# Two PSUM copies per pass of an expert loop go from ScalarE to VectorE (one Trainium2 core)

## What is computed

```python
S, R, M, K = (8, 16, 64, 4)          # 8 groups, rank 16, 64 experts per group, 4 chosen
z = jnp.einsum('nd,sdr->nsr', xf, P)
scores = jnp.einsum('nsr,smr->nsm', z, C)      # 8 x 64 = 512 scores per row
topv, topi = jax.lax.top_k(scores, K)
w = jax.nn.softmax(topv, axis=-1)
h = jax.nn.gelu(jnp.einsum('nsr,nskrh->nskh', z, W1g) + b1g)
yl = jnp.einsum('nskh,nskhr->nskr', h, W2g) + b2g
comb = jnp.einsum('nskr,nsk->nsr', yl, w)
out = jax.nn.gelu(comb @ G1 + g1b) @ G2 + g2b
```

## Time and profile before

| what | value |
|---|---|
| median of 3 runs | 939.27 us (939.06 to 944.86) |
| the profiled execution, its own time | 939.98 us |
| its span (first to last instruction) | 938.2 us, so 1.8 us lie around it |
| granted TensorE clock, mean | 0.981 of full speed |
| PE busy | 881.2 us, 94% |
| DVE busy | 670.1 us, 71% |
| ACT busy | 592.1 us, 63% |
| POOL busy | 478.7 us, 51% |

### The profile page before, as it was taken

How to read it: one execution, slowest core, us unless ns; L and a number is a source line. 1 busy time by engine, 2 the same in 40 slices (tenths; PEclk the granted TensorE clock), 3 DMA queues, 4 the chain that set the end, 5 groups by cost and what they waited for, 6 DMA issues and landing times.

```text
span 938.2 us, 16131 instructions
## 1 busy us (share of the span) xinstructions
PE 881.2 (94%) x5408; PEld 397.9 (42%) x5408; DVE 670.1 (71%) x1678; ACT 592.1 (63%) x871; POOL 478.7 (51%) x448
## 2 busy tenths in 40 slices
PE   8799999999999968899989998999999999999997
PEld 3477777777777756122222222222222222222222
DVE  5566666665675866777787878787878887877774
ACT  1121211223333245788898999899989998988784
POOL 0335353334243517477766666666656665665453
PEclk9999999999999988699999999999999999999999
DMA  9500000000000166966878798878788987899772
GB/s 250 219 1 1 1 37 36 1 1 1 1 1 21 39 112 107 257 227 212 237 243 241 233 253 252 250 243 252 229 266 227 264 236 239 245 259 288 234 254 101
DMA packets 89804, 154.14 MB, mean 164 GB/s; under 512 B 30211, under 2 KB 56068, under 8 KB 89329
## 3 DMA queue, kind: packets, MB, share of 16 engines
q1 hardware_dynamic: 88750, 149.86, 53.1%
q10 hardware_dynamic: 972, 3.24, 2.7%
HBM read 138.81 MB, written 15.83 MB: 165 GB/s over the span
## 4 chain that ended last, share of the span: by engine, by line
PE 71%; DVE 11%; ACT 11%; issue 4%; DMA 1%; POOL 1%; SPq 0%; ACTq 0%; DVEq 0%; POOLq 0%
PE ps L797 15%; PE ps L734 14%; PE ps L450 8%; PE ps L458 5%; PE ps L523 4%; PE ps L773 4%; PE ps L515 3%; DVE ring L1557 3%; PE ps L532 3%; DVE ring L1560 3%; PE ps L574 2%; PE ps L493 2%; PE ps L545 2%; ACT ring L1105 2%; ACT ring L1112 2%
## 5 line engine op out<-in xcount | busy, mean ns | idle before, releaser
L1761 POOL TENSOR_TENSOR ring<-ring,wbc 128x512 f32<-128x512 f32 x192 | 244.9, 1281 | 155.4 <-ACT ring L1112 137.9
L1557 DVE TENSOR_TENSOR ring<-ps,ring 128x1024 f32<-128x1024 f32 x192 | 234.6, 1222 | 92.5 <-ACT ring L1105 50.8
L734 PE MATMUL ps<-zst,w1st 99*128 99x512 bf16 x768 | 218.7, 389 | 23.0 <-ACT ring L1105 15.0
L797 PE MATMUL ps<-ring,w2cur 128*32 128x512 f32 x1536 | 204.8, 606 | 0.0
L1105 ACT ACTIVATE ring<-ps 128x1024 f32<-128x1024 f32 x192 | 197.3, 1027 | 6.4 <-PE ps L734 6.2
L1616 POOL TENSOR_TENSOR t<-t 128x768 f32<-128x768 f32 x48 | 87.4, 1833 | 187.7 <-DVE t L1243 187.7
L1114 ACT ACTIVATE ps<-ps 128x512 f32<-128x512 f32 x192 | 114.1, 594 | 45.1 <-PE ps L734 44.8
L1560 DVE TENSOR_TENSOR ring<-ps,wbc 128x512 f32<-128x512 f32 x192 | 130.9, 682 | 2.2 <-DMA wbc<-w_rows 2.2
L734 PEld LDWEIGHTS ps<-zst,w1st 99*128 99x128 bf16 x768 | 60.2, 98 | 162.4 <-issue 36.8
L1241 DVE TENSOR_TENSOR t<-ps,rope 128x768 f32<-128x768 f32 x48 | 45.7, 952 | 104.7 <-PE ps L458 68.5
L1112 ACT ACTIVATE ring<-ps 128x512 f32<-128x512 f32 x192 | 115.6, 602 | 0.3 <-PE ps L734 0.3
(11 more groups left out here) (169 smaller groups left out, 1153.6 us busy)
## 6 DMA issues: line engine op xcount, KB each, us to landing
wbc<-w_rows SPq DMA_DIRECT2D x192, 512.0 KB, 5.2
w2cur<-in_w SPq DMA_DIRECT2D x48, 256.0 KB, 5.0
w_parts<-wp SPq DMA_DIRECT2D x72, 64.0 KB, 3.3
zst<-z_parts SPq DMA_DIRECT2D x72, 64.0 KB, 5.3
w1st<-w_parts ACTq DMA_DIRECT2D x12, 256.0 KB
wst<-w_parts SPq DMA_DIRECT2D x24, 128.0 KB, 4.5
z_parts<-zp SPq DMA_DIRECT2D x6, 384.0 KB, 5.0
wst<-w_parts SPq DMA_DIRECT2D x24, 96.0 KB, 4.7
```

The source lines that it names most:

```text
L734: return pe.matmul(bank(to), w1st[0:99, 4 * a + j, col:col + P], zst[0:99, (i // 2) % 2, j, :], start=True, stop=True)
L797: mm = pe.matmul(bank(YBANK, 0, 512, 32 * j, 32 * j + 32), w2cur[:, n, j, :], ring[:, (4 * g + j) % RING, :], start=False, stop=(n == 7 an ...
L1557: dve.tensor_tensor(v, ps[:, WBANK * 512:WBANK * 512 + 1024], v, ALU.mult).then_inc(s["duo_done"], 1)
L1761: pool.tensor_tensor(ring[:, slot, :], ring[:, slot, :], wbc[:, g % 4, 1, :], ALU.mult).then_inc(s["tri_done"], 1)
```

## The change

Both copies are removed from ScalarE's loop. In VectorE's loop the scores of the next tile are copied at n = 4 and the transposed weights at n = 6, each behind the two products of the group, and the weights' copy ahead of `largest`. The waits of the copies go with them. What runs before the loop (tiles 0 to 5) keeps its copies on ScalarE.

```diff
@@ ScalarE's loop @@
                                ACT.Gelu_apprx_tanh).then_inc(s["duo_gelu"], 1)
-                if n == 6 and tile < TILES:
-                    keep_gates(tile, PBANK)
                 if g >= 18 and g % 16 == 2:
...
                     ln_root(5, 12, 24)
-                if n == 4 and tile + 1 < TILES:
-                    copy_scores(tile + 1, PBANK)
@@ VectorE @@
+            def copy_scores(tile, at):
+
+                dve.wait_ge(s["s_full"], tile + 1)
+                dve.wait_ge(s["t_mr"], LENT + tile)
+                dve.wait_ge(s["p_dist"], LENT + tile)
+                dve.tensor_copy(sc[:, :, 0:M], bank(at).rearrange("p (s m) -> p s m", m=M)).then_inc(s["s_copied"], 1)
+
+            def keep_gates(tile, at):
+
+                dve.wait_ge(s["t_full"], tile + 1)
+                if tile >= 8:
+                    dve.wait_ge(s["r_stored"], 32 * (tile - 7))
+                    dve.wait_ge(s["lo_done"], LENT + tile - 7)
+                dve.tensor_copy(gates_of(tile), bank(at).rearrange("p (g n) -> p g n", g=4)).then_inc(s["wT_done"], 1)
@@ VectorE's loop @@
                     normaliser(tile)
+                if n == 4 and tile + 1 < TILES:
+                    copy_scores(tile + 1, PBANK)
+                if n == 6 and tile < TILES:
+                    keep_gates(tile, PBANK)
                 if n in (5, 6) and tile + 1 < TILES:
                     largest(tile + 1, 4 * (n - 5), 4 * (n - 4))
```

## The result

| | before | changed |
|---|---|---|
| median | 942.07 us (939.06 to 945.04, 4 runs) | 958.42 us (956.64 to 959.94, 4 runs) |
| profiled execution, span | 939.98 us, 938.2 us | 958.0 us, 956.2 us |
| DVE / ACT busy | 670.1 / 592.1 us | 696.8 / 574.9 us |

The ratio is 1.0174, 95% interval [1.0134, 1.0214]: slower by 16.3 us, where +0.7% was forecast. The direction was right, the size was not, and the range (up to 951.5) was missed.

What follows compares the result with a forecast made beforehand. TensorE was taken as the bound, with VectorE setting the pace from group 7 to 1. Costs by pass, 4.1 + 1.4 + 0.2 + 0.8 - 0.25 = 6.2 us, gave a median of 945.5 us (+0.7%), range 938.5 to 951.5.

Steps and rivals of the forecast that it cites:

- The bounds: TensorE bounds except at three waits; from group 7 to 1 VectorE works back to back and sets the pace.
- Part 1, what ScalarE gives: Without ScalarE's copies, TensorE's matmuls lose waits of 0.12 us at group 4 and 0.27 at group 6 per plain pass.
- The copy's duration and pitch: A moved 128x512 copy on VectorE: 0.68 us long, 0.60 from start to start, bounds 0.33 and 0.74.
- The group 4 copy: Score copy behind line 1560 of group 4, hidden in 0.59 us of VectorE idle time: cost 0.
- The signs by busy time: Signs of a right forecast: ScalarE's busy time down by 21.9 us, VectorE's up by about 37 x 0.68 = 25.
- The sum by kinds of pass: Costs added over the loop's plain, pre-`first_final`, early and last passes: 6.2 us in all.
- the passes up to a `first_final`: Passes 4, 8, 12 and 16, where VectorE catches up behind the first wait: 0.35 us each, 1.4 in all.
- pass 0's 0.8: Pass 0, group 4: two small additional VectorE operations leave too little idle time; estimated at twice a plain pass, 0.8 us.
- Pass 18: VectorE idles 1.05 us at group 6 and takes the copy free; TensorE keeps its gain: -0.25 us.
- the group 6 item of part 2: Gate copy ahead of the maxima on VectorE adds 0.60 us, so line 1557 of group 7 starts 0.41 late.
- The GpSimd item: `high_part` starts at the copy's end, 572.9, and group 7's product is 0.36 us late, needed over 3 us later: cost 0.
- Clearly slower: Rival: relief doesn't reach VectorE at group 6 and the group 4 copy shows, or all copies are bare: 950.7 to 961.5, chance 0.09.

Runs made afterwards that it cites:

- e1_again: Second run of the changed kernel with VectorE's small top4 copy written as a tensor_reduce over an axis of one element: 951.13 us, ratio 1.0099.
- e3: The changed kernel with the group 6 gate copy back on ScalarE, so only the group 4 score copy is on VectorE: ratio 0.9987.
- before_again: The kernel before, unchanged, run once more for a second profile: ratio 1.0028 to the kernel before.
- e8: e1_again's kernel with TensorE's idle gap ahead of group 4 of passes 3, 7, 11 and 15 filled by repeated score matmuls: 949.03 us, ratio 1.0072.
- after_again: The changed kernel, unchanged, run a second time beside e1_again: 956.10 us, ratio 1.0159.
- e7: e3's kernel with ScalarE's group 6 gate copy moved behind the tri gelu: 955.39 us, ratio 1.0133.
- e5: The changed kernel with GpSimd's high_part moved from group 6 to group 7, ahead of low_parts: ratio 1.0189.
- e12: e7's kernel with the small copy as a tensor_reduce and the idle gap of passes 3, 7, 11 and 15 filled: 936.56 us, ratio 0.9934.

## Why the prediction was wrong

By its own steps:

- **The bounds: right.** VectorE sets the pace from group 7 to group 1. With the reduce (e1_again) TensorE gives the relief back ahead of `duo_gates` of group 0, 0.50 us, and 0.2 us behind it; the forecast had `two_first` of groups 0 and 2.
- **Part 1, what ScalarE gives: right.** 0.12 us per plain pass at group 4 (e3: 22.20 - 22.09 = 0.11), 0.27 at group 6 (1.31 to 1.04). The latter reached nobody, as said.
- **The copy's duration and pitch: right.** 0.68 and 0.60 us. The group 4 copy costs nothing (e3). The signs by busy time say less than they seem to. VectorE's came out near the forecast (26.7 against 25) by luck: 37 x 0.68 counts overlaps twice, and the small copy filled the difference. ScalarE's fell by 17.2 and not 21.9 us, since each copy overlaps its neighbour there too (37 x the 0.48 of part 1 is 17.8).
- **The sum by kinds of pass: right, once the small copy is out of it.** In e1_again a plain pass is 0.41 us longer than before (forecast 0.41); the passes up to a `first_final` 25.36 against 25.01, 0.35 (0.35). Passes 0 to 3 came to 0.4 us in all (25.76, 25.76, 25.76 and 22.96 against 25.77, 25.76, 25.76 and 22.56), where 1.0 was forecast; pass 0's 0.8 was a guess and too high. Pass 18 gives 0.27 back (18.29 against 18.56 in before_again; forecast 0.25). Passes with a half-clock stretch left out, the differences add up to 5.6 us, where 6.2 was forecast. The times say it less exactly: e1_again is +1.0%, and e8 meets the forecast's +0.7% (1.0072) with a filled gap that the forecast knew nothing of, which is in part luck.
- **The step that failed** is in the group 6 item of part 2: "Then the copy's 0.60, then the maxima. Line 1557 of group 7 starts at 573.33 - 0.19 + 0.60 = 573.74, 0.41 late." It carried every other VectorE operation over with its old duration, a term put at nothing without a reason. The small copy between the maxima and that product went from 0.18 to 0.70 us, and the pass from +0.41 to +0.93. The GpSimd item looked only at queues and semaphores ("Cost: 0"): it had `high_part` start at the copy's end, and didn't ask what VectorE does 0.55 us later, when the subtraction starts. With the forecast's own numbers the meeting was there to find, and its price too: the same copy beside a GpSimd product takes 0.50 us at 359.83 in the trace of before. Before, GpSimd's cast starts at 572.58 and its subtraction at 573.06, 0.48 later; with the gate copy's end at 572.9 that gives a subtraction at about 573.4. Before, the small copy starts 0.63 us behind the maxima (573.03 against 572.40); with the maxima at 572.81 that gives 573.44, some 0.05 us behind the subtraction.
- **No rival held it.** "Clearly slower" covers the size (950.7 to 961.5) by another mechanism, waits ahead of the copies, which cost nothing: the copies start with no idle time. That it had a chance of 0.09 is no merit of the reasoning.

What the 16.3 us consist of, by these runs: about 6 the forecast steps (5.6 by the passes; e8 against before, 949.03 - 943.12 = 5.9), and 5 to 6.6 the small copy (e1_again against after_again, 5.0; the durations, 6.6). The 4 to 5 us that are left are not settled. Half-clock stretches may be part of it (from e1_again to e8 2.1 us, within the noise). So may what lies ahead of pass 1: in the two first profiles the loop begins 3.4 us apart, at 379.4 and 382.8, with no code changed ahead of it, and from pass 0 to pass 1 the changed kernel has a fall (27.31 us against 25.77). The base also moved: the kernel before had 939.27 us over the three runs on which the forecast stands, 942.07 with a fourth, and 941.9 to 943.9 in all later sets. The forecast missed against either.

## What to carry to other kernels

When work moves between engines, redo the timeline of GpSimd beside VectorE's and not only the queues: look for a VectorE copy from SBUF to SBUF, however small, that would start while GpSimd runs a product, and charge it with the rest of GpSimd's instruction. Here a copy of 32 elements on a path with no slack was better written as a reduce over an axis of one. Where two instructions meet within 0.03 us, as here, a small shift can tip the time, also a shift that only makes something earlier (e7).

## What the runs showed of the hardware that was not expected

- The small VectorE copy SBUF to SBUF (128x32 fp32) that starts while GpSimd runs a product of two SBUF operands ends 0.03 to 0.07 us behind that product's end. This holds in all 80 such cases of the 17 traces: 0.68 us beside the rest of a 1.28 us product (e5), 1.27 beside a whole one (e7). Started 0.03 us ahead of GpSimd, it takes 0.18 (before). Where GpSimd's start reads up to 0.01 us earlier, it took 0.70 in 35 of 45 cases and 0.18 in ten. A tensor_reduce of the same data takes 0.19 in all 91 such coincidences. The copies out of PSUM (0.65 to 0.69) and the maxima were never lengthened. The Trainium skill, "SBUF — State Buffer", section "SBUF: two separate sides", gives VectorE and GpSimd a shared pair of ports that whichever starts first holds for its whole instruction, and counts VectorE's 2-port perf modes among its users. The trace agrees for the side that VectorE loses.
- GpSimd loses as well where VectorE starts first, and VectorE's products of two SBUF operands take part. In the kernel before, ahead of the loop, both engines run the same 128x768 product. GpSimd's takes 1.80 us alone and 2.58 when it starts 0.04 us behind VectorE's; VectorE's takes 0.96 there, and 2.47 when it starts 0.15 us behind GpSimd's (360.41). GpSimd's timeline:

```profile
353.00 2.58 POOL L1628 TENSOR_TENSOR oT_b<-oT_b,gate_b 128x768 f32<-128x768 f32 x1 [5.02 <-DVE oT_b L1351]
...
357.38 1.80 POOL L1628 TENSOR_TENSOR oT_b<-oT_b,gate_b 128x768 f32<-128x768 f32 x1
```

- The granted clock fell to the lower level between 0.1 us before and 1.6 us after TensorE's restart from an idle gap of 1.8 us, for 3.4 or 6.8 us, in 17 of 39 gaps (passes 7, 11 and 15); with the gap filled in none of 12. One fall, in pass 4 of e12, had no such gap ahead of it.
